# A two-layer graph kernel on one Trainium2 core: another order of ScalarE's work within a step, and the expert product one step later

## The chip, the cores and the metric

The kernel runs on one core of a Trainium2 chip. The metric is the device time in microseconds (us) from launch to end. The profile also gives a span, from the first to the last instruction of one profiled execution. Engines are named as in the profile: PE (matmul), DVE, ACT, POOL, and SP, which issues nearly all DMAs.

## The reference, cut to what matters

Inputs: x of 8 x 1024 x 512, adj of 8 x 1024 x 1024, all float32. The routing picks one of four experts for each of the 8 graphs.

```python
# layer 0
diff = (adj[..., None] - mean_relation) ** 2                 # 4 kernels
w = exp(-0.5 * diff / (1e-14 + precision_relation ** 2))
w = w / sum(w, axis=-1, keepdims=True)                       # over the 4 kernels
ws = sum(w, axis=2)                                          # over the row
x = layernorm(x + reshape(einsum('bknd,nod->bkno', ws[..., None] * x[:, :, None, :], W)))
# layer 1
top1 = argmax(x.mean(axis=1) @ router_w + router_b)
out = einsum('bnm,bmk->bnk', adj, einsum('bnh,bhk->bnk', x, expert_w[top1]))
# batch norm of out with the sums of all graphs that share an expert, gamma, beta, relu
x = layernorm(x + relu(batchnorm(out)))
```

## The kernel before, in words

The 8 graphs have 8 tiles of 128 rows each, so there are 64 tiles (`TILES`). A first part goes through steps n = 0 to `LAST` - 1. Every engine has its own loop over n with the same step numbers, and semaphores alone tie the loops together. In step n:

- SP loads the adj tile n+2 and the x tile n+3, transposes tile n+1 of adj by DMA, stores a finished unit of the expert product from `o_stage` and transposes tile n+2 of x. At a graph's first unit it also loads the chosen expert into `w_sel`.
- POOL cuts the adj tile n+1 and the x tile n+2 into a high and a low float16 half (`pool_al`: adj is cut) and, every second step, normalizes two rows of tiles of x1 (`norm_pair`).
- ACT computes for tile n the squared distances to the four kernels (L513): three into `wgt` and one, SOLO, in place over the adj tile. `weigh_others` takes the exponential of the three in one instruction (L519), `weigh_solo` that of SOLO into the PSUM area `tot` (L524). `sum_reciprocal(n-1)` turns the sum over the four kernels of tile n-1, in the same `tot`, into its reciprocal by a logarithm (L528) and an exponential (L530). ACT also copies two matmul results out of PSUM: a unit of z (L552) and a unit of o (L566).
- DVE: `sums(n)` adds the three weights to `tot` (L781, three instructions). `row_sums(n-1)` multiplies by the reciprocal and sums the rows (L749, three instructions). `weighted(n-1)` adds x and the product h (L768). `low_z` makes the low half of a z unit after ACT's copy (L721), `y_stats`/`y_mean_var` and `o_stats` are statistics (L727, L733, L738).
- PE: `h_product(n)` (12 matmuls), `z_product(n-10)` (24 matmuls; z is adj times x1, 64 units with unit u needing all rows of its graph) and `o_product(n - O_LAG)` (12 matmuls; z times the expert). `z_product(u)` may start when the low half of unit u-2 is made (`dve_z`), `o_product(u)` when unit u-1 was copied out (`act_o`).

`tot` exists once. So `sums(n)` must be finished before `sum_reciprocal(n)`, that before `row_sums(n)`, and that before `weigh_solo(n+1)` and `sums(n+1)`.

After step 63 no adj tiles are left, and PE works off the rest: units 54 to 63 of z and what is left of o. I call this the drain. The last 64 - `KEPT` units of o stay in SBUF, the others go to DRAM (`out_spill`) and come back. When all of o is there, the batch norm constants are made, and a last part goes over the graphs: relu, transposition on PE, addition and layer norm.

Each line number in this text is the one of this kernel.

Of the kernel before, what the change touches and what calls it, by code (L numbers as in the profile page):

```python
# [37 lines left out]
Z_LAG = 10  # L38
O_LAG = 14

# [7 lines left out]
def gnn_program(nc, x, adj, mean_rel, prec_rel, w0, router_w, router_b, expert_w, gamma, beta, x1_spill,  # L48
# [14 lines left out]
    with ExitStack() as ctx:  # L63
# [193 lines left out]
        def _(sp):  # L257
# [54 lines left out]
            for n in range(LAST):  # L312
# [18 lines left out]
                if n + 1 < TILES:  # L331
                    turn_adj(n + 1)
                if 0 <= u - 1 < KEPT:
                    half, k = (u - 1) % T // G, (u - 1) % G
                    sp.wait_ge(act_o, u)
                    dst = out_spill.rearrange("b (c p) n -> b c p n", p=P)[(u - 1) // T, k, :, half * HALF:(half + 1) * HALF]
                    sp.dma_start(dst, o_stage[:, k % 2, :]).then_inc(o_stored[k % 2], 16)
# [14 lines left out]
            def fetch_o(n):  # L352
                i, b = n % RING, batch_of(n)
                if n == 1:

                    sp.wait_ge(o_stored[0], KEPT // 2 * 16 + 16)
                    sp.wait_ge(dve_ws, NK * (TILES - 1))
                    for half in (slice(0, HALF // 2), slice(HALF // 2, HALF)):
                        sp.dma_start(o_chunk(i, 0)[:, half], out_spill[b, 0:P, half]).then_inc(o_back[i], 16)
                elif 1 < n < NB:  # L360
                    if n < RING:

                        sp.wait_ge(pe_z, TILES - T if n == 2 else TILES)
                        if n == 5:

                            sp.wait_ge(pe_h, TILES)
                            sp.wait_ge(pe_o, TILES)
                    else:

                        sp.wait_ge(pe_back, (n - RING + 1) * T)  # L370
                        wait(sp, *landed(o_back, n - RING))

                    for k in range(2):
                        sp.wait_ge(o_stored[k], (b + 1) * T * 8)
                    for h in range(2):
                        src = out_spill.rearrange("b (h c p) n -> b h p c n", h=2, p=P)[b, h]
                        sp.dma_start(o_buf[i][h], src).then_inc(o_back[i], 16)
# [120 lines left out]
        def _(act):  # L498
# [33 lines left out]
            for n in range(LAST):  # L532
# [7 lines left out]
                if 1 <= n <= 2 * E:  # L540
                    e, part_ = expert_half(n - 1)
                    act.wait_ge(experts_landed[e], 16)
                    s.activation(planes(e)[:, 0, part_], expert_in(e)[:, part_], ACT.Copy, scale=W_SCALE).then_inc(act_whi, 1)
                u = n - Z_LAG - 1
                if 0 <= u < TILES:
# [9 lines left out]
                if 0 <= u < TILES:  # L555
# [10 lines left out]
                    s.activation(out_unit(u), ps_out(u), ACT.Copy, scale=1.0 / (Z_SCALE * W_SCALE)).then_inc(act_o, 1)  # L566
                if 0 <= n - 1 < TILES:
                    sum_reciprocal(n - 1)
                if n < TILES:
                    weigh_others(n)  # L570
                    act.wait_ge(pool_al, n + 1)
                    square(n, SOLO, adj_in[:, n % ADJ_RING, :])
                    weigh_solo(n)
# [12 lines left out]
            def relu(n, chunks):  # L586

                i, b = n % RING, batch_of(n)
                if chunks[0] == 0:
                    wait(act, act_o, TILES if n < 2 else 0)  # L590
                    wait(act, *landed(o_back, n))
                pieces = [slice(0, NR)]
# [42 lines left out]
        def _(dve):  # L635
# [147 lines left out]
            for n in range(LAST):  # L783
                if 0 <= n - 2 < TILES:
                    y_stats(n - 2)
                if 0 <= n - Z_LAG - 1 < TILES:
                    low_z(n - Z_LAG - 1)
                if 0 <= n - 2 < TILES:
                    y_mean_var(n - 2)
                if 0 <= n - O_LAG - 1 < TILES:  # L790
                    o_stats(n - O_LAG - 1)
                if 1 <= n <= 2 * E:
# [223 lines left out]
```

## Time and profile before

| | us |
|---|---|
| median of 3 runs | 925.3 (924.48 to 925.61) |
| profiled execution, its own time | 928.54 |
| its span | 926.6 |
| busy in the span: PE, DVE, ACT, POOL | 766.6, 783.0, 799.0, 633.5 |

A busy time says how long an engine had an instruction in work. It does not say which engine the others waited for. That is read from the order of the instructions in one step, where an instruction that had to wait starts right after the end of the one that released it.

### The profile page before, as it was taken

The page shows a single profiled execution, that of the slowest core. Times are in us where ns is not written, and L with a number is a line of the kernel's source. Part 1 is how long each engine was busy: PE and PEld are TensorE (multiplying, and loading weights), DVE is VectorE, ACT ScalarE, POOL GpSimd, SP SyncE. Part 2 cuts the span into 40 slices and gives each one's busy share as a digit, 9 for nine tenths or more (in the row PEclk, how much of TensorE's full clock was granted, in tenths as well). Part 3 has the DMA queues.
Part 4 walks back from the last instruction along what each step waited for, and adds up shares of the span by engine and source line. Part 5 has one row for each costly group of instructions (what it writes and reads, how often), then busy time and mean ns, then how long its engine had stood idle before and what let it go on. Part 6 is the DMA issues. An engine that isn't in the chain of part 4 may idle for free.

```text
span 926.6 us, 12505 instructions
## 1 busy us (share of the span) xinstructions
PE 766.6 (83%) x3922; PEld 362.6 (39%) x3922; DVE 783.0 (84%) x1702; ACT 799.0 (86%) x789; POOL 633.5 (68%) x712
## 2 busy tenths in 40 slices
PE   1445468899999999999999999999999899956652
PEld 1111123344444444444444344444444343425442
DVE  2999988999999999999999999999999712139995
ACT  4999989899999999999999999999999311139997
POOL 7499999999888888888888888888884400000000
PEclk8766679899999999999999999999999989987776
DMA  8599887888797779777877888898763003598896
GB/s 247 150 284 250 184 232 177 218 210 203 197 235 186 182 187 245 201 198 203 208 189 194 222 210 188 199 242 195 191 164 99 1 1 134 198 401 322 295 383 228
DMA packets 262676, 191.17 MB, mean 206 GB/s; under 512 B 210002, under 2 KB 210258, under 8 KB 261074
## 3 DMA queue, kind: packets, MB, share of 16 engines
q1 hardware_dynamic: 262322, 190.38, 74.8%
q8 instruction: 31, 0.51, 0.2%
q14 instruction: 35, 0.29, 0.1%
q10 hardware_dynamic: 288, 0.00, 0.0%
HBM read 91.52 MB, written 48.50 MB: 151 GB/s over the span
## 4 chain that ended last, share of the span: by engine, by line
DVE 49%; ACT 17%; POOL 16%; PE 10%; issue 5%; DMA 2%; SPq 0%; DVEq 0%; POOLq 0%; ACTq 0%
DVE wgt L749 19%; DVE ps_t L781 18%; DVE x_in L768 6%; PE ps_z L929 5%; ACT ps_t L530 4%; ACT ps_t L528 4%; POOL adj_cut L429 3%; PE ps_o L945 3%; POOL x_turn L440 2%; POOL adj_in L424 2%; POOL x1p L466 2%; POOL adj_cut L427 2%; ACT adjT L614 2%; PE ps_t L945 2%; DMA w_sel<-w_planes 1%
## 5 line engine op out<-in xcount | busy, mean ns | idle before, releaser
L929 PE MATMUL ps_z<-adjT,x1p 128*128 128x512 f16 x1536 | 346.5, 383 | 0.0
L914 PE MATMUL ps_h<-w0T,x_turn 128*128 128x512 f16 x768 | 196.3, 410 | 76.9 <-DVE x_in L768 54.1
L781 DVE TENSOR_TENSOR ps_t<-ps_t,wgt 128x1024 f32<-128x1024 f32 x192 | 235.9, 1229 | 15.0 <-ACT ps_t L524 10.6
L749 DVE SCALAR_TENSOR_TENSOR wgt<-wgt,ps_t 128x1024 f32<-128x1024 f32 x192 | 224.8, 1215 | 18.1 <-ACT ps_t L530 17.9
L929 PEld LDWEIGHTS ps_z<-adjT,x1p 128*128 128x128 f16 x1536 | 150.8, 99 | 183.0 <-issue 7.1
L513 ACT ACTIVATE wgt<-adj_in,neg_mu 128x1024 f32<-128x1024 f32 x192 | 205.6, 1134 | 5.5 <-issue 5.4
L519 ACT ACTIVATE wgt<-wgt 128x3072 f32<-128x3072 f32 x64 | 176.5, 2758 | 0.0
L945 PE MATMUL ps_o<-zT,w_sel 128*128 128x512 f16 x684 | 159.9, 384 | 6.2 <-DMA w_sel<-w_planes 6.1
L914 PEld LDWEIGHTS ps_h<-w0T,x_turn 128*128 128x128 f16 x768 | 76.1, 103 | 186.5 <-issue 94.0
L429 POOL TENSOR_TENSOR adj_cut<-adj_in,adj_cut 128x1024 f16<-128x1024 f32 x64 | 136.6, 2134 | 5.3
L492 POOL TENSOR_TENSOR r_nmr<-r_mv,r_std 128x4 f32<-128x4 f32 x16 | 3.2, 199 | 170.7 <-ACT r_std L607 170.7
L945 PEld LDWEIGHTS ps_o<-zT,w_sel 128*128 128x128 f16 x684 | 67.2, 99 | 89.8 <-DMA w_sel<-w_planes 8.7
L424 POOL TENSOR_SCALAR adj_in<-adj_in 128x1024 f32<-128x1024 f32 x64 | 68.7, 1073 | 22.0 <-DMA adj_in<-in_adj_dram 16.9
L552 ACT ACTIVATE zT<-ps_z 128x512 f16<-128x512 f32 x64 | 36.9, 577 | 52.5 <-PE ps_z L929 52.5
L768 DVE SCALAR_TENSOR_TENSOR x_in<-ps_h,wsum,x_in 128x128 f32<-128x128 f32 x256 | 72.6, 344 | 8.9
L721 DVE SCALAR_TENSOR_TENSOR zT<-ps_z,zT 128x512 f16<-128x512 f32 x64 | 43.3, 676 | 43.4 <-ACT zT L552 43.4
L466 POOL TENSOR_TENSOR x1p<-x_in,x1p 128x512 f16<-128x512 f32 x64 | 76.1, 1190 | 5.3
L440 POOL TENSOR_TENSOR x_turn<-x_in,x_turn 128x512 f16<-128x512 f32 x64 | 75.2, 1175 | 5.3
L528 ACT ACTIVATE ps_t<-ps_t 128x1024 f32<-128x1024 f32 x64 | 64.6, 1010 | 10.7 <-DVE ps_t L781 8.7
L513 ACT ACTIVATE adj_in<-adj_in,neg_mu 128x1024 f32<-128x1024 f32 x64 | 72.8, 1138 | 0.0
L427 POOL TENSOR_SCALAR adj_cut<-adj_in 128x1024 f16<-128x1024 f32 x64 | 67.6, 1057 | 5.3
L524 ACT ACTIVATE ps_t<-adj_in 128x1024 f32<-128x1024 f32 x64 | 65.8, 1028 | 2.8 <-DVE wgt L749 0.6
(164 smaller groups left out, 864.0 us busy)
## 6 DMA issues: line engine op xcount, KB each, us to landing
adj_in<-in_adj_dram SPq DMA_DIRECT2D x64, 512.0 KB, 4.0
x_in<-in_x_dram SPq DMA_DIRECT2D x64, 256.0 KB, 4.4
x_spill<-x_in SPq DMA_DIRECT2D x28, 512.0 KB, 3.3
out_spill<-o_stage SPq DMA_DIRECT2D x49, 256.0 KB, 3.0
w_sel<-w_planes SPq DMA_DIRECT2D x8, 1024.0 KB, 6.0
adjT<-x_spill SPq DMA_DIRECT2D x6, 1024.0 KB, 9.6
out_dram<-adjT SPq DMA_DIRECT2D x6, 1024.0 KB, 12.0
adjT<-out_spill SPq DMA_DIRECT2D x4, 1024.0 KB, 9.9
```

What stands on the lines that cost most here:

```text
L429: g.tensor_tensor(cut[:, 1, :], tile, cut[:, 0, :], ALU.subtract).then_inc(pool_al, 1)
L440: g.tensor_tensor(cut[:, 1, :], tile, cut[:, 0, :], ALU.subtract).then_inc(pool_xl, 1)
L466: g.tensor_tensor(x1p[:, b % 2, 1, t, :], row, x1p[:, b % 2, 0, t, :], ALU.subtract).then_inc(pool_1l, 1)
L513: s.activation(to, adj_in[:, n % ADJ_RING, :], ACT.Square, bias=neg_mu[:, k:k + 1], scale=spread[k]).then_inc(act_sq, 1)
L519: s.activation(w, w, ACT.Exp, scale=-1.0).then_inc(act_w, 1)
L528: s.activation(tot, tot, ACT.Ln, scale=SUM_SCALE).then_inc(act_ln, 1)
L749: v.scalar_tensor_tensor(out=wgt[:, m % 2, j, :], in0=wgt[:, m % 2, j, :], scalar=SUM_SCALE / W0_SCALE, in1=tot, op0=ALU.mult, op1=ALU.mul ...
L768: last = v.scalar_tensor_tensor(out=row[:, f], in0=ps_h[:, m % 2, f], scalar=wsum[:, m % 2, COLUMN[k]:COLUMN[k] + 1], in1=row[:, f], op0=A ...
L781: v.tensor_tensor(tot, tot, wgt[:, n % 2, j, :], ALU.add).then_inc(dve_tot, 1)
L914: last = te.matmul(ps_h[:, n % 2, :], xT[:, n % 2, left, c, :], w0T[:, right, c, :], start=(c + i == 0), stop=(c == C - 1 and i == 2))
L929: last = te.matmul(ps_z[:, u % 2, :], x1p[:, b % 2, left, t, k * P:(k + 1) * P], adjT[:, b % 2, right, t, half * HALF:(half + 1) * HALF], ...
L945: last = te.matmul(ps_out(u), w_sel[:, left, c, k * P:(k + 1) * P], zT[:, right, half, c, :], start=(c + i == 0), stop=(c == C - 1 and i = ...
```

## The change

ACT's order within a step becomes: the four squares (SOLO's among them, with its wait for `pool_al`), the logarithm and exponential of `sum_reciprocal(n-1)`, the exponential of the three kernels, the copies of z and o, and the exponential of SOLO, which opens the next tile's sum. `O_LAG` is 15 in place of 14, so that PE, ACT and DVE handle a unit of o one step later, the loop has one more step, and `KEPT` is 48 in place of 49. DVE makes the low half of z and the statistics of o one step later again. SP stores a unit of o one step later relative to its copy. Unit 48 of o stays in SBUF, so the small fetch of `fetch_o(1)` goes away.

```diff
-O_LAG = 14
+O_LAG = 15
...
-                if 0 <= u - 1 < KEPT:
-                    half, k = (u - 1) % T // G, (u - 1) % G
-                    sp.wait_ge(act_o, u)
+                if 0 <= u - 2 < KEPT:
+                    half, k = (u - 2) % T // G, (u - 2) % G
+                    sp.wait_ge(act_o, u - 1)
...
-                if n == 1:
-
-                    sp.wait_ge(o_stored[0], KEPT // 2 * 16 + 16)
-                    sp.wait_ge(dve_ws, NK * (TILES - 1))
-                    for half in (slice(0, HALF // 2), slice(HALF // 2, HALF)):
-                        sp.dma_start(o_chunk(i, 0)[:, half], out_spill[b, 0:P, half]).then_inc(o_back[i], 16)
-                elif 1 < n < NB:
+                if 1 < n < NB:
...
+                if n < TILES:
+                    act.wait_ge(pool_al, n + 1)
+                    square(n, SOLO, adj_in[:, n % ADJ_RING, :])
+                if 0 <= n - 1 < TILES:
+                    sum_reciprocal(n - 1)
+                if n < TILES:
+                    weigh_others(n)
                 u = n - Z_LAG - 1
...
                     s.activation(out_unit(u), ps_out(u), ACT.Copy, scale=1.0 / (Z_SCALE * W_SCALE)).then_inc(act_o, 1)
-                if 0 <= n - 1 < TILES:
-                    sum_reciprocal(n - 1)
                 if n < TILES:
-                    weigh_others(n)
-                    act.wait_ge(pool_al, n + 1)
-                    square(n, SOLO, adj_in[:, n % ADJ_RING, :])
                     weigh_solo(n)
...
-                if 0 <= n - Z_LAG - 1 < TILES:
-                    low_z(n - Z_LAG - 1)
+                if 0 <= n - Z_LAG - 2 < TILES:
+                    low_z(n - Z_LAG - 2)
                 if 0 <= n - 2 < TILES:
                     y_mean_var(n - 2)
-                if 0 <= n - O_LAG - 1 < TILES:
-                    o_stats(n - O_LAG - 1)
+                if 0 <= n - O_LAG - 2 < TILES:
+                    o_stats(n - O_LAG - 2)
```

ACT's queue in the middle of the first part before, one step (the numbers behind L are lines, the arrow goes from what is read to what is written):

```order
L513 ACTIVATE wgt<-adj_in,neg_mu 128x1024 x3
L552 ACTIVATE zT<-ps_z 128x512
L566 ACTIVATE o_stage<-ps_o 128x512
L528 ACTIVATE ps_t<-ps_t 128x1024
L530 ACTIVATE ps_t<-ps_t 128x1024
L519 ACTIVATE wgt<-wgt 128x3072
L513 ACTIVATE adj_in<-adj_in,neg_mu 128x1024
L524 ACTIVATE ps_t<-adj_in 128x1024
```

The same place in the changed kernel, whose lines have other numbers (L506 is the square, L521 and L523 the pair of `sum_reciprocal`, L512 the exponential of three kernels, L517 that of SOLO):

```order
L506 ACTIVATE wgt<-adj_in,neg_mu 128x1024 x3
L506 ACTIVATE adj_in<-adj_in,neg_mu 128x1024
L521 ACTIVATE ps_t<-ps_t 128x1024
L523 ACTIVATE ps_t<-ps_t 128x1024
L512 ACTIVATE wgt<-wgt 128x3072
L552 ACTIVATE zT<-ps_z 128x512
L566 ACTIVATE o_stage<-ps_o 128x512
L517 ACTIVATE ps_t<-adj_in 128x1024
```

The two copies moved from ahead of the pair L528/L530 to behind the large exponential, and SOLO's square from behind that exponential to ahead of the pair.

PE's queue at the end of the first part before, from the second last z product (L929) to the last o product (L945); the fourth row is unit 59 of o:

```order
L929 MATMUL ps_z<-adjT,x1p 128x512 x24
L945 MATMUL ps_o<-zT,w_sel 128x512 x12
L929 MATMUL ps_z<-adjT,x1p 128x512 x24
L945 MATMUL ps_t<-zT,w_sel 128x512 x12
L945 MATMUL ps_o<-zT,w_sel 128x512 x12
L945 MATMUL ps_t<-zT,w_sel 128x512 x12
L945 MATMUL ps_o<-zT,w_sel 128x512 x12
L945 MATMUL ps_t<-zT,w_sel 128x512 x12
```

The same stretch in the changed kernel, where the z product is L924 and the o product L940:

```order
L924 MATMUL ps_z<-adjT,x1p 128x512 x24
L940 MATMUL ps_t<-zT,w_sel 128x512 x12
L924 MATMUL ps_z<-adjT,x1p 128x512 x24
L940 MATMUL ps_o<-zT,w_sel 128x512 x12
L940 MATMUL ps_t<-zT,w_sel 128x512 x12
L940 MATMUL ps_o<-zT,w_sel 128x512 x12
L940 MATMUL ps_t<-zT,w_sel 128x512 x12
L940 MATMUL ps_o<-zT,w_sel 128x512 x12
L940 MATMUL ps_t<-zT,w_sel 128x512 x12
```

Behind the last z product there are now six products of o (units 58 to 63) instead of five.

## Rows read from the trace of the kernel before

**Rows 1.** The page, section 4: the chain that ended last, by engine.

```profile
DVE 49%; ACT 17%; POOL 16%; PE 10%; issue 5%; DMA 2%; SPq 0%; DVEq 0%; POOLq 0%; ACTq 0%
```

**Rows 2.** Windows, 400:700. Busy us (instructions) of the engines, PEclk, DMA.

```profile
core 0: us, PE busy (x) PEld busy (x) DVE busy (x) ACT busy (x) POOL busy (x), PEclk, DMA share, GB/s
400.00:700.00 300.00, 291.89 (x1536) 132.41 (x1535) 287.15 (x596) 296.03 (x274) 263.81 (x288) 1.00 0.80 199
```

**Rows 3.** Timeline of DVE: start, duration, line, tiles, idle before.

```profile
204.25 3.76 DVE L781 TENSOR_TENSOR ps_t<-ps_t,wgt 128x1024 f32<-128x1024 f32 x3
...
210.12 1.22 DVE L749 SCALAR_TENSOR_TENSOR wgt<-wgt,ps_t 128x1024 f32<-128x1024 f32 x1 [0.25 <-ACT ps_t L530]
...
212.41 1.22 DVE L749 SCALAR_TENSOR_TENSOR wgt<-wgt,ps_t 128x1024 f32<-128x1024 f32 x1
...
215.20 3.76 DVE L781 TENSOR_TENSOR ps_t<-ps_t,wgt 128x1024 f32<-128x1024 f32 x3
```

**Rows 4.** Timeline of ACT, step 17.

```profile
203.84 3.21 ACT L513 ACTIVATE wgt<-adj_in,neg_mu 128x1024 f32<-128x1024 f32 x3
206.96 0.57 ACT L552 ACTIVATE zT<-ps_z 128x512 f16<-128x512 f32 x1
207.44 0.58 ACT L566 ACTIVATE o_stage<-ps_o 128x512 f32<-128x512 f32 x1
208.04 1.01 ACT L528 ACTIVATE ps_t<-ps_t 128x1024 f32<-128x1024 f32 x1
...
212.66 1.14 ACT L513 ACTIVATE adj_in<-adj_in,neg_mu 128x1024 f32<-128x1024 f32 x1
213.83 1.03 ACT L524 ACTIVATE ps_t<-adj_in 128x1024 f32<-128x1024 f32 x1
```

**Rows 5.** Timeline of ACT, steps 9, 11, 15 and 16.

```profile
112.76 3.23 ACT L513 ACTIVATE wgt<-adj_in,neg_mu 128x1024 f32<-128x1024 f32 x3
116.86 1.01 ACT L528 ACTIVATE ps_t<-ps_t 128x1024 f32<-128x1024 f32 x1 [0.86 <-DVE ps_t L781]
...
140.24 0.60 ACT L552 ACTIVATE zT<-ps_z 128x512 f16<-128x512 f32 x1 [2.47 <-PE ps_z L929]
140.73 1.02 ACT L528 ACTIVATE ps_t<-ps_t 128x1024 f32<-128x1024 f32 x1
...
185.43 0.60 ACT L566 ACTIVATE o_stage<-ps_o 128x512 f32<-128x512 f32 x1 [1.10 <-PE ps_o L945]
185.92 1.02 ACT L528 ACTIVATE ps_t<-ps_t 128x1024 f32<-128x1024 f32 x1
...
196.59 0.60 ACT L566 ACTIVATE o_stage<-ps_o 128x512 f32<-128x512 f32 x1 [0.22 <-PE ps_o L945]
```

**Rows 6.** Timeline of DVE: the sums of tiles 10 and 14.

```profile
134.97 3.76 DVE L781 TENSOR_TENSOR ps_t<-ps_t,wgt 128x1024 f32<-128x1024 f32 x3
...
181.05 3.76 DVE L781 TENSOR_TENSOR ps_t<-ps_t,wgt 128x1024 f32<-128x1024 f32 x3
```

**Rows 7.** Timeline of POOL: last cut instruction of adj tiles 9 and 17.

```profile
113.94 2.14 POOL L429 TENSOR_TENSOR adj_cut<-adj_in,adj_cut 128x1024 f16<-128x1024 f32 x1
...
197.96 2.13 POOL L429 TENSOR_TENSOR adj_cut<-adj_in,adj_cut 128x1024 f16<-128x1024 f32 x1
```

**Rows 8.** Timeline of PE: unit 0 of o, then the drain.

```profile
181.21 4.18 PE L945 MATMUL ps_o<-zT,w_sel 128*128 128x512 f16 x12 [2.95 <-DMA w_sel<-w_planes]
...
713.19 5.34 PE L929 MATMUL ps_z<-adjT,x1p 128*128 128x512 f16 x24
718.37 2.75 PE L945 MATMUL ps_o<-zT,w_sel 128*128 128x512 f16 x12
720.96 5.34 PE L929 MATMUL ps_z<-adjT,x1p 128*128 128x512 f16 x24
...
740.50 1.01 PE L905 MATMUL ps_s<-ones_h,x1p 128*128 128x1 f16 x32 [3.83 <-POOL x1p L466]
741.37 8.26 PE L929 MATMUL ps_z<-adjT,x1p 128*128 128x512 f16 x24
```

**Rows 9.** Timeline of DVE, step 64: the low half of z.

```profile
725.45 0.67 DVE L721 SCALAR_TENSOR_TENSOR zT<-ps_z,zT 128x512 f16<-128x512 f32 x1
```

More of the change, by code:

```diff
@@ L332, in _ @@
                     turn_adj(n + 1)
-                if 0 <= u - 1 < KEPT:
-                    half, k = (u - 1) % T // G, (u - 1) % G
-                    sp.wait_ge(act_o, u)
-                    dst = out_spill.rearrange("b (c p) n -> b c p n", p=P)[(u - 1) // T, k, :, half * HALF:(half + 1) * HALF]
+                if 0 <= u - 2 < KEPT:
+                    half, k = (u - 2) % T // G, (u - 2) % G
+                    sp.wait_ge(act_o, u - 1)
+                    dst = out_spill.rearrange("b (c p) n -> b c p n", p=P)[(u - 2) // T, k, :, half * HALF:(half + 1) * HALF]
                     sp.dma_start(dst, o_stage[:, k % 2, :]).then_inc(o_stored[k % 2], 16)
@@ L370, in fetch_o @@
                         sp.wait_ge(pe_back, (n - RING + 1) * T)
-                        wait(sp, *landed(o_back, n - RING))
                     for k in range(2):
@@ L590, in relu @@
                     wait(act, act_o, TILES if n < 2 else 0)
-                    wait(act, *landed(o_back, n))
+                    wait(act, o_back[i], n // RING * 32 if n % RING < 2 else 32)
                 pieces = [slice(0, NR)]
```

## The prediction, made before the changed kernel ran

> **What bounds the kernel now.** I began with the chain that ended last: nearly half of it is DVE, with ACT and POOL behind it [rows 1]. The windows view says why the shares alone don't decide: in 300 us of the middle, ACT is busy 296.03, PE 291.89 and DVE 287.15 us, at full granted clock [rows 2]. Three engines are nearly full, so the question is which of them the step's length comes from. I took the order within one step.
>
> The sums on `tot` start at 204.25 and the next ones at 215.20 [rows 3], a step of 10.95 us. Between them lies a ring: sums to the start of the logarithm, 208.04 - 204.25 = 3.79 [rows 3, 4]; the pair L528/L530 until the row sums start, 210.12 - 208.04 = 2.08; row sums and `weighted` until the next sums, 215.20 - 210.12 = 5.08. That makes 10.95 with nothing left over. The small DVE jobs (L727, L721, L733, L738) lie in the 2.08 us in which DVE waits for the reciprocal anyway; 0.25 us of them is still idle [rows 3].
>
> ACT is only just faster. After the copy of o the logarithm starts 208.04 - 207.44 = 0.60 later. Where nothing holds it, it starts 185.92 - 185.43 = 0.49 after the same copy [rows 5]. So ACT waits 0.11 us per step for DVE's sums, and its own ring would be 10.84. PE needs 5.18 for z (718.37 - 713.19) and 2.59 for 12 matmuls (720.96 - 718.37) [rows 8], so 10.36 for h, z and o.
>
> Outside the steady steps there are two places of interest. In steps 11, 15 and 16 ACT waits 2.47, 1.10 and 0.22 for PE before a copy, ahead of the logarithm [rows 5]. In the drain PE alone sets the time.
>
> **The change, part by part.**
>
> *The steady step.* With four squares ahead of it, ACT reaches the logarithm after four pitches of 3.12 / 3 = 1.04 (206.96 - 203.84 is three of them), at 203.84 + 4.16 = 208.00. Today it starts at 208.04, held by the sums that end at 204.25 + 3.76 = 208.01 [rows 3, 4]. Nothing moves. Behind the pair, the two copies (about 0.97 us) take the place of SOLO's square (213.83 - 212.66 = 1.17), so SOLO's exponential could start 0.2 earlier. It is held by the third row sum, which ends at 212.41 + 1.22 = 213.63, and the next sums wait for `weighted`, not for it: it ends at 213.83 + 1.03 = 214.86 and they start at 215.20 [rows 3, 4]. Cost 0. The ring contains no ACT instruction that became shorter.
>
> The 1.17 against 1.04 is worth a look. A square followed by an instruction that reads its result has 0.13 more pitch than a square followed by an unrelated one [rows 4]. The Trainium skill (ScalarE: Activation LUTs, section "What ACT_TABLE_LOAD costs") says that back-to-back ACTIVATEs overlap by about 93 ns, and the trace agrees (duration 1.14, pitch 1.04). By that rule an order without the dependent neighbours would save about 0.1 us in each of 64 steps, some 6 us as an estimate from the Trainium skill; this would count only if ACT set the step.
>
> *The wait for `pool_al`, now earlier.* SOLO's square of tile n now starts 3.12 us into the step. In step 9 that is 112.76 + 3.12 = 115.88, and POOL's cut of tile 9 ends at 113.94 + 2.14 = 116.08 [rows 5, 7]. ACT starts the square at about 116.13, the logarithm at 117.17 instead of 116.86: 0.3 us lost, since this logarithm had followed DVE directly. By step 17 the cut ends at 200.09 and the square is due at 206.96 [rows 4, 7], 6.9 us later, or 3.9 if ACT runs 3 us earlier than today. No further wait.
>
> *The copies, now late in the step.* In step 11 the logarithm starts at 140.73, though the sums of tile 10 had ended by 134.97 + 3.76; with today's latency of 0.03 it could start at 138.76 [rows 5, 6]. In the new order the copy of z comes over 4.5 us later in the step than today, long after PE has delivered. Gain 1.97. In step 15: 185.92 against 181.05 + 3.79 = 184.84, gain 1.08. In step 16 the wait of 0.22 gives about 0.20. Together 3.25; less the 0.3 of step 9, 2.95 us, carried to the end of the first part.
>
> *Low half of z one step later.* `z_product(n-10)` now waits for `low_z(n-12)` in DVE's step n, which ends between the sums' end, 208.01, and the row sums' start, 210.12 [rows 3]; by its place, second of the four small jobs, near 209.2. That is about 2 us behind the place of z in PE's step today. PE's order becomes h, wait, z, o. Once shifted, it needs 10.36 of 10.95 us per step, so it falls behind no further; the small matmuls of routing are inside the 291.89 of 300 us [rows 2]. z runs from 209.2 to 214.4, and its copy comes in ACT's next step, behind the large exponential at about 213.7 + 10.95 - 1.1 = 223.5: 9 us in hand. The o product would start at 214.4, and the copy of o that it waits for ends about when SOLO's exponential starts, at 213.7: 0.7 us to spare, and a miss would cost PE only, which has 0.59 more. Cost 0.
>
> *SP's queue.* The load of `w_sel` moves to an odd step and waits for the last o product of the old graph, which ends about 2 us later in the step; behind it stand the transposes of adj and x and the store of o. The adj transposes are mostly held by POOL's cut anyway, and the store's wait is relaxed by the extra lag. In step 14 PE waited 2.95 us for this load [rows 8]; unit 0 now has a later step. Its gain is that of step 15 above. In the drain, load and product keep their distance. The removed fetch of unit 48 was issued in the drain, long ahead of the last part's second graph, which uses it. Cost 0.
>
> *The drain.* PE makes one o product fewer before step 64 and one more behind it: +2.59 [rows 8]. Against that stands the stall at unit 56 of z, which needs the last rows of x1: PE idles 3.83 us and then takes 8.26 instead of 5.34 for 24 matmuls, 2.92 more [rows 8]. In today's times: z 53 would start some 2 us later than 713.19, by the shift above, so that o 48 ends at 715.3 + 5.18 + 2.59 = 723.1, and z 54 waits for `low_z(52)`, which stands where the low half of unit 53 stands today and ends at 725.45 + 0.67 = 726.12 [rows 9]. PE idles 3 us there. What does the clock do? After an idle of 2.95 us the 12 matmuls at 181.21 took 4.18 instead of 2.75, 1.43 more; after 3.83 us the 24 at 741.37 took 2.92 more [rows 8]. The first is the nearer row in idle time, the second in what runs; I take 1.7. Then z 54 ends at 726.2 + 5.18 + 1.7 = 733.1, o 49 at 735.7, z 55 at 740.9, o 50 at 743.4. The last rows of x1 arrive at 740.5, so there is no idle left at unit 56: routing sums 0.8, z 56 from 744.3 to 749.4. Today it ends at 749.5. The stall is used up by PE's own delay, and the extra product stays: +2.55. With no loss of clock it is 2.55 - 1.7 = +0.85; with 2.92 it is +3.77.
>
> *Last part.* Unchanged. Its first fetches stand in SP's queue behind the last load of `w_sel`, which waits for one o product more (2.59 us), and that load itself lies ahead of ten products more, so they are hidden.
>
> *Sum.* -2.95 + 2.55 = -0.4 us on the span of 926.6, so 926.2. The profiled execution's own time was 928.54, 3.2 above the median of 925.3; the same difference on the median gives **924.9**. Within 0.2% (1.85 us) a measurement of this kernel cannot tell it from no change.
>
> **The rivals.**
>
> *B, the clock holds in the drain.* Then -2.95 + 0.85 = -2.1, 923.2: faster by 0.23%. Against it: an idle of the same length did cost clock at 181.21. For it: 291.89 of 300 us around gaps of 0.6 us show no loss at all [rows 2], and how deep the fall goes differs between my two rows. 16 in 100.
>
> *C, ACT sets the step.* Then 0.13 us less in each of about 62 steps, 8 us, so 925.3 - 0.4 - 8 = 917. This is the case in which the Trainium skill's rule on overlap would decide. Against it: the 0.11 us that ACT waits before the logarithm, and the ring that closes without it. 5 in 100.
>
> *D, PE falls behind (slower).* PE now starts each z behind `low_z` in the same step. Should the idle before z cost clock as at 181.21, a step of PE would be 10.36 + 1.43 = 11.8 us; beyond 10.95 it would first use the 9 us in hand, then set the step: 47 steps by 0.85, less 9, some +30 us, 955. It decides once PE needs more than 10.95. Against it: the spare time per step is only moved, not enlarged. 5 in 100.
>
> *E, the early gain does not come (slower).* POOL is only 0.2 us late in step 9 and cuts at its own pace; if in steps 12 to 16 its cuts, or PE's first z units, hold ACT again, the 3 us are lost and only the drain's term remains: +2.55, 927.9. It needs cuts 2 us later than today's. 10 in 100.
>
> **How the numbers follow.** Forecast 62, B 16, C 5, D 5, E 10; 2 for something faster that I don't see. The forecast's own range, by the drain's bounds, is -2.1 to +0.8. The range that leaves out C, D and half of E, with part of the 1.1 us between the three runs: 922.8 to 927.2. Of the forecast's 62, 60 lie within 0.2%. Faster: B 16, C 5, 2, and 1 of the forecast: 24. Slower: D 5, E 10, 1 of the forecast: 16. Same: 60.
>
> **What the changed profile would show.** Steps of 10.95 us in the middle, as before; no ACT idle before the copies in steps 11, 15, 16, and the squares of step 17 near 200.9 instead of 203.84; a short wait for POOL in step 9; PE waiting for L721's successor before z in most steps; an idle of about 3 us before z 54 and slow matmuls behind it, none before z 56; the last o product ending about 0.4 us earlier than today. Steps shorter than 10.95 would prove C, longer ones D; an end of the first part that is not 3 us earlier, E; a z 54 of 5.3 us, B.

## The result and the profile after

| | before | after |
|---|---|---|
| median (us) | 925.32 (4 runs) | 930.75 (4 runs) |
| ratio to before, 95% interval | | 1.006 (1.0043 to 1.0078) |
| profiled execution, own time | 928.54 | 930.31 |
| its span | 926.6 | 928.4 |

The change made the kernel 5.4 us slower. The forecast was 924.9, between 922.8 and 927.2. It was wrong: the kernel became slower, and by more than the range allowed.

The profiled execution of before that the forecast used spent 3.4 us more in its drain than a second one, profiled later (below). Against that second one the difference of the spans, 5.6 us, is close to the difference of the medians, 5.4. In the table T(n) is the start of SOLO's exponential of tile n, and the drain goes from T(63) to the end of the last o product:

| | before, second profile | after | difference | predicted |
|---|---|---|---|---|
| T(8) | 111.38 | 117.13 | **+5.75** | 0 |
| T(8) to T(17) | 102.09 | 98.86 | **-3.23** | -2.95 |
| T(17) to T(63) | 505.95 | 506.25 | +0.30 | 0 |
| drain | 98.66 | 101.34 | **+2.68** | +2.55 |
| last part | 104.72 | 104.82 | +0.10 | 0 |
| span | 922.8 | 928.4 | +5.6 | -0.4 |

Two of the three large terms came out near the forecast (how much of that was luck is said below). The third, +5.75 up to step 8, was not in the forecast at all. The next rows show where it is made. This is ACT's timeline of the changed kernel in step 2: start, duration, line, operation, and in brackets the idle time ahead of it with what ended it. In the changed kernel L506 are the squares, L521 and L523 the logarithm pair, L512 the large exponential, L517 that of SOLO.

```profile
34.77 1.03 ACT L517 ACTIVATE ps_t<-adj_in 128x1024 f32<-128x1024 f32 x1 [0.97 <-DVE wgt L744]
35.73 3.22 ACT L506 ACTIVATE wgt<-adj_in,neg_mu 128x1024 f32<-128x1024 f32 x3
38.85 1.04 ACT L536 ACTIVATE x1p<-adjT 128x1024 f16<-128x1024 f32 x1
39.80 1.14 ACT L506 ACTIVATE adj_in<-adj_in,neg_mu 128x1024 f32<-128x1024 f32 x1
40.84 1.00 ACT L521 ACTIVATE ps_t<-ps_t 128x1024 f32<-128x1024 f32 x1
41.88 1.01 ACT L523 ACTIVATE ps_t<-ps_t 128x1024 f32<-128x1024 f32 x1
42.80 2.75 ACT L512 ACTIVATE wgt<-wgt 128x3072 f32<-128x3072 f32 x1
46.52 1.03 ACT L517 ACTIVATE ps_t<-adj_in 128x1024 f32<-128x1024 f32 x1 [0.97 <-DVE wgt L744]
```

DVE's timeline of the changed kernel in the same step (L776 sums, L744 row sums):

```profile
36.25 3.76 DVE L776 TENSOR_TENSOR ps_t<-ps_t,wgt 128x1024 f32<-128x1024 f32 x3
...
40.73 1.19 DVE L790 SCALAR_TENSOR_TENSOR x1p<-adjT,x1p 128x1024 f16<-128x1024 f32 x1
42.91 1.22 DVE L744 SCALAR_TENSOR_TENSOR wgt<-wgt,ps_t 128x1024 f32<-128x1024 f32 x1 [0.99 <-ACT ps_t L523]
```

And ACT's timeline of the kernel before in this step:

```profile
35.33 3.21 ACT L513 ACTIVATE wgt<-adj_in,neg_mu 128x1024 f32<-128x1024 f32 x3
38.44 1.04 ACT L543 ACTIVATE x1p<-adjT 128x1024 f16<-128x1024 f32 x1
39.53 1.01 ACT L528 ACTIVATE ps_t<-ps_t 128x1024 f32<-128x1024 f32 x1
40.58 1.01 ACT L530 ACTIVATE ps_t<-ps_t 128x1024 f32<-128x1024 f32 x1
```

In steps 1 to 8 ACT and DVE have one more job. The weights of the four experts are cut into a high and a low float16 part, which I call planes, in two halves per expert: ACT makes the high half (L543 before, L536 after, 1.04 us), DVE the low one, and SP stores the finished planes in `w_planes`. ACT's part stood ahead of the logarithm already. The change puts SOLO's square there too. So five ACT instructions run between the start of the step's squares and the logarithm, 40.84 - 35.73 = 5.11 us, while DVE's sums are done at 36.25 + 3.76 = 40.01. The logarithm is 0.83 late. Row sums, `weighted` and the next sums all follow from it. Nothing fills the place that the square left: ACT idles 0.97 behind the large exponential. The step is 46.52 - 34.77 = 11.75 us instead of 10.95, and the other seven lose 0.7 to 0.9 each. (T(8) shows 5.75 and not the 6.35 that these eight add up to, because tile 0 began 0.60 earlier in this execution, T(0) 21.11 against 21.71.)

Outside these steps the forecast holds. ACT's timeline of the changed kernel in step 11, in step 16, and in a step of the middle (these answer to [rows 5] and [rows 4]):

```profile
148.91 0.59 ACT L552 ACTIVATE zT<-ps_z 128x512 f16<-128x512 f32 x1
149.98 1.03 ACT L517 ACTIVATE ps_t<-adj_in 128x1024 f32<-128x1024 f32 x1 [0.49 <-DVE wgt L744]
...
203.96 0.59 ACT L552 ACTIVATE zT<-ps_z 128x512 f16<-128x512 f32 x1
204.44 0.60 ACT L566 ACTIVATE o_stage<-ps_o 128x512 f32<-128x512 f32 x1
205.04 1.03 ACT L517 ACTIVATE ps_t<-adj_in 128x1024 f32<-128x1024 f32 x1
...
401.83 0.58 ACT L552 ACTIVATE zT<-ps_z 128x512 f16<-128x512 f32 x1
402.30 0.60 ACT L566 ACTIVATE o_stage<-ps_o 128x512 f32<-128x512 f32 x1
402.90 1.03 ACT L517 ACTIVATE ps_t<-adj_in 128x1024 f32<-128x1024 f32 x1
```

No copy waits for PE any more. PE's timeline of the changed kernel, in the middle and in the drain (answers to [rows 8]):

```profile
409.36 5.35 PE L924 MATMUL ps_z<-adjT,x1p 128*128 128x512 f16 x24 [0.21 <-DVE zT L716]
...
728.71 7.04 PE L924 MATMUL ps_z<-adjT,x1p 128*128 128x512 f16 x24 [2.79 <-DVE zT L716]
...
745.94 0.94 PE L900 MATMUL ps_s<-ones_h,x1p 128*128 128x1 f16 x32
746.75 5.34 PE L924 MATMUL ps_z<-adjT,x1p 128*128 128x512 f16 x24
...
792.33 2.76 PE L940 MATMUL ps_o<-zT,w_sel 128*128 128x512 f16 x12 [0.57 <-DMA w_sel<-w_planes]
```

z waits a little for the low half in the middle. z 54 starts after an idle of 2.79 and takes 7.04 instead of 5.34, 1.70 more (the granted clock is 0.54 in its first 3.5 us, near the lower level of 1.2 GHz); the forecast had 3 us and 1.7. Ahead of z 56 there is no idle left (it was 3.83).

### The profile page after: what moved, and what is told of

Read it like the earlier page. It is cut to its first block, busy times and chain, and to the rows that moved or that the text cites. A ratio compares the mean times of both kernels' runs of the same rounds, so it can differ in the third digit from the quotient of the medians.

```text
span 928.4 us, 12501 instructions
## 1 busy us (share of the span) xinstructions
PE 766.2 (83%) x3922; PEld 361.0 (39%) x3922; DVE 784.3 (84%) x1702; ACT 798.8 (86%) x789; POOL 634.5 (68%) x712
## 4 chain that ended last, share of the span: by engine, by line
DVE 53%; ACT 19%; POOL 10%; PE 10%; issue 6%; DMA 1%; DVEq 0%; ACTq 0%; POOLq 0%; SPq 0%
DVE wgt L744 21%; DVE ps_t L776 20%; DVE x_in L763 6%; PE ps_z L924 5%; ACT ps_t L523 5%; ACT ps_t L521 5%; PE ps_t L940 2%; POOL adj_cut L422 2%; PE ps_o L940 2%; ACT adjT L609 2%; POOL x_turn L433 1%; POOL adj_cut L420 1%; ACT x_in L609 1%; POOL adj_in L417 1%; ACT wgt L593 1%
## 5 line engine op out<-in xcount | busy, mean ns | idle before, releaser
L924 PE MATMUL ps_z<-adjT,x1p 128*128 128x512 f16 x1536 | 345.8, 382 | 20.6 <-DVE zT L716 20.4
L909 PE MATMUL ps_h<-w0T,x_turn 128*128 128x512 f16 x768 | 197.6, 412 | 74.7 <-DVE x_in L763 59.5
L776 DVE TENSOR_TENSOR ps_t<-ps_t,wgt 128x1024 f32<-128x1024 f32 x192 | 235.9, 1229 | 14.8 <-ACT ps_t L517 10.4
L744 DVE SCALAR_TENSOR_TENSOR wgt<-wgt,ps_t 128x1024 f32<-128x1024 f32 x192 | 224.8, 1216 | 22.6 <-ACT ps_t L523 22.6
L924 PEld LDWEIGHTS ps_z<-adjT,x1p 128*128 128x128 f16 x1536 | 146.9, 98 | 212.7 <-DVE zT L716 40.8
L506 ACT ACTIVATE wgt<-adj_in,neg_mu 128x1024 f32<-128x1024 f32 x192 | 205.8, 1136 | 5.9 <-issue 5.9
L512 ACT ACTIVATE wgt<-wgt 128x3072 f32<-128x3072 f32 x64 | 176.5, 2759 | 0.0
L940 PE MATMUL ps_o<-zT,w_sel 128*128 128x512 f16 x672 | 154.2, 379 | 0.6 <-DMA w_sel<-w_planes 0.6
L909 PEld LDWEIGHTS ps_h<-w0T,x_turn 128*128 128x128 f16 x768 | 78.0, 104 | 180.9 <-issue 91.2
L940 PEld LDWEIGHTS ps_o<-zT,w_sel 128*128 128x128 f16 x672 | 65.6, 98 | 80.1 <-DMA w_sel<-w_planes 1.1
L417 POOL TENSOR_SCALAR adj_in<-adj_in 128x1024 f32<-128x1024 f32 x64 | 67.0, 1047 | 21.0 <-DMA adj_in<-in_adj_dram 15.8
L517 ACT ACTIVATE ps_t<-adj_in 128x1024 f32<-128x1024 f32 x64 | 65.8, 1028 | 13.7 <-DVE wgt L744 12.4
L506 ACT ACTIVATE adj_in<-adj_in,neg_mu 128x1024 f32<-128x1024 f32 x64 | 72.7, 1136 | 0.0
L521 ACT ACTIVATE ps_t<-ps_t 128x1024 f32<-128x1024 f32 x64 | 64.5, 1008 | 8.0 <-DVE ps_t L776 5.8
## 6 DMA issues: line engine op xcount, KB each, us to landing
out_dram<-adjT SPq DMA_DIRECT2D x6, 1024.0 KB, 11.3
```

What stands on the lines that cost most here:

```text
L506: s.activation(to, adj_in[:, n % ADJ_RING, :], ACT.Square, bias=neg_mu[:, k:k + 1], scale=spread[k]).then_inc(act_sq, 1)
L512: s.activation(w, w, ACT.Exp, scale=-1.0).then_inc(act_w, 1)
L521: s.activation(tot, tot, ACT.Ln, scale=SUM_SCALE).then_inc(act_ln, 1)
L744: v.scalar_tensor_tensor(out=wgt[:, m % 2, j, :], in0=wgt[:, m % 2, j, :], scalar=SUM_SCALE / W0_SCALE, in1=tot, op0=ALU.mult, op1=ALU.mul ...
L776: v.tensor_tensor(tot, tot, wgt[:, n % 2, j, :], ALU.add).then_inc(dve_tot, 1)
L909: last = te.matmul(ps_h[:, n % 2, :], xT[:, n % 2, left, c, :], w0T[:, right, c, :], start=(c + i == 0), stop=(c == C - 1 and i == 2))
```

## The experiments

All medians stand beside runs of the kernel before on the same chip, 925.3 to 925.9. T(n) and the drain are as above and those of the profiled execution.

**The kernel before, profiled a second time.**

> The kernel before, unchanged, looked at once more. The profiled execution that the prediction used took 928.5 us, 3.2 above the median; in its drain PE waited 2.2 us for the last w_sel load and then ran the o product in 4.25 us. Theory 1: this wait and the slow stretch behind it come and go with the landing time of the load, so another look whose own time is near 925.3 shows an idle under 1 us there and an o product of about 2.75. Rival: the 3.2 us lie elsewhere (start or last part), and the wait is 2.2 us again.

Median 925.34. Its profile shows the drain at 98.66 instead of 102.04: the wait for the last `w_sel` was 0.88 instead of 2.21, and the o product behind it took 2.76 instead of 4.25. Step 11 waited 3.72 for PE, and steps 15 and 16 not at all; the total of the three, 3.79 in the forecast's trace, is about the same. The start and the last part differ by less than 0.5 us, so the rival has fallen.

**SOLO's square late in steps 0 to 8** (from the changed kernel).

```diff
-                if n < TILES:
+                if 2 * E < n < TILES:
                     act.wait_ge(pool_al, n + 1)
                     square(n, SOLO, adj_in[:, n % ADJ_RING, :])
...
                     weigh_others(n)
+                if n <= 2 * E:
+                    act.wait_ge(pool_al, n + 1)
+                    square(n, SOLO, adj_in[:, n % ADJ_RING, :])
```

> The changed kernel, but in steps 0 to 8 the square of SOLO stands behind the large exponential again, as before. Theory 1 (the loss is the pile of three squares, half an expert plane and SOLO's square ahead of the logarithm in steps 1 to 8): steps 1 to 8 are 10.95 us again instead of 11.75, the whole is 5.4 us below the changed kernel, at 925.3, ratio to before about 1.000. Rival (the earlier wait for POOL's cut in these steps holds ACT, or the longer lag costs all of it in the drain): no more than 1 us below the changed kernel, ratio 1.005 or more.

Median 924.06, ratio 0.9979 (0.9963 to 0.9995). ACT's timeline of this kernel in step 2:

```profile
39.09 1.04 ACT L536 ACTIVATE x1p<-adjT 128x1024 f16<-128x1024 f32 x1
40.18 1.01 ACT L521 ACTIVATE ps_t<-ps_t 128x1024 f32<-128x1024 f32 x1
...
45.96 1.03 ACT L517 ACTIVATE ps_t<-adj_in 128x1024 f32<-128x1024 f32 x1
```

The steps are 10.95 again (45.96 - 35.01), T(8) is 112.07, T(63) 717.23: 5.0 earlier than in the changed kernel, and the median 6.7 lower, more than the 5.4 expected. With the one place mended, the change is 1.3 us faster than before. Both rivals have fallen.

**SOLO's square early in steps 1 to 8** (from the kernel before, nothing else changed).

```diff
+                if 1 <= n <= 2 * E:
+                    act.wait_ge(pool_al, n + 1)
+                    square(n, SOLO, adj_in[:, n % ADJ_RING, :])
...
                 if 0 <= n - 1 < TILES:
                     sum_reciprocal(n - 1)
                 if n < TILES:
                     weigh_others(n)
-                    act.wait_ge(pool_al, n + 1)
-                    square(n, SOLO, adj_in[:, n % ADJ_RING, :])
+                    if not 1 <= n <= 2 * E:
+                        act.wait_ge(pool_al, n + 1)
+                        square(n, SOLO, adj_in[:, n % ADJ_RING, :])
```

> The kernel before, with one part of the change alone: in steps 1 to 8 SOLO's square stands ahead of the logarithm. Theory 1: 0.8 us more in each of the eight steps, less 0.6 for a wait in step 8 that the kernel before has anyway: 5.4 us at the end of step 8; some of it may be hidden in step 11, where ACT waits 2.5 us for PE, if PE is not pushed back with it. So 928.5 to 930.7, ratio 1.0035 to 1.006. Rival (the loss comes from the lag): ratio 1.000.

Median 928.28, ratio 1.0028 (1.0012 to 1.0044). T(8) is 117.71, the loss in full, so the rival, the lag, didn't make it. But T(63) is only 3.2 later than in the second profile of before. ACT's timeline of this kernel in step 11:

```profile
143.79 0.57 ACT L555 ACTIVATE zT<-ps_z 128x512 f16<-128x512 f32 x1
144.87 1.01 ACT L528 ACTIVATE ps_t<-ps_t 128x1024 f32<-128x1024 f32 x1 [0.51 <-DVE ps_t L785]
```

The copy of z waits for nothing: PE's first z had time to finish while ACT was late. PE's timeline shows it, first of the kernel before (second profile), then of this one (L905 and L909 are the sums for the routing, which need the same last rows of x1 as z 0):

```profile
132.21 1.01 PE L905 MATMUL ps_s<-ones_h,x1p 128*128 128x1 f16 x32 [3.36 <-POOL x1p L466]
133.08 8.05 PE L929 MATMUL ps_z<-adjT,x1p 128*128 128x512 f16 x24
```

```profile
135.44 1.02 PE L909 MATMUL ps_s<-ones_h,x1p 128*128 128x1 f16 x32
136.32 5.34 PE L933 MATMUL ps_z<-adjT,x1p 128*128 128x512 f16 x24
```

Before, PE idled for POOL's last rows of x1 and then ran z 0 at a granted clock of 0.50 (133 to 136 us), until 141.13. Here z 0 starts 3.2 later, without that idle, takes 5.34 and ends at 141.66, only 0.5 later, while ACT is 6.3 later. So the loss and the gain are not two independent things. The wait of step 11 absorbs about 3 us of the delay made before it, and where a delay has already hidden it, removing the wait brings almost nothing: T(63) is 722.59 here and 722.24 in the changed kernel.

**The lags alone** (the changed kernel with ACT's old order).

```diff
-                if n < TILES:
-                    act.wait_ge(pool_al, n + 1)
-                    square(n, SOLO, adj_in[:, n % ADJ_RING, :])
-                if 0 <= n - 1 < TILES:
-                    sum_reciprocal(n - 1)
-                if n < TILES:
-                    weigh_others(n)
...
+                if 0 <= n - 1 < TILES:
+                    sum_reciprocal(n - 1)
                 if n < TILES:
+                    weigh_others(n)
+                    act.wait_ge(pool_al, n + 1)
+                    square(n, SOLO, adj_in[:, n % ADJ_RING, :])
                     weigh_solo(n)
```

> The changed kernel with ACT's order of before: only the lag of 15 and the later low halves and statistics are left. Theory 1: steps 1 to 8 at 10.95 us; the wait of step 11 is back (2.5 us), those of steps 15 and 16 stay away (-1.3); drain +2.6: together +1.3 us against before, 926.6, ratio 1.001. Rival (the lag and the later low half of z cost most of the 5.4 us): 929 or more, ratio 1.004 or more.

Median 927.62, ratio 1.0021 (1.0006 to 1.0035). ACT's timeline of this kernel:

```profile
140.58 0.60 ACT L545 ACTIVATE zT<-ps_z 128x512 f16<-128x512 f32 x1 [2.67 <-PE ps_z L922]
...
196.48 0.60 ACT L559 ACTIVATE o_stage<-ps_o 128x512 f32<-128x512 f32 x1 [0.86 <-PE ps_o L938]
```

T(63) is 719.91, as before, and the drain 101.17: the lags alone cost the drain its 2.5 us and nothing else, and the waits for PE stay. The expectation had those of steps 15 and 16 gone; one of 0.86 stayed, and the time is 1.0 above the 926.6 expected. So ACT's order is what removes these waits, and what makes the loss.

**Step 11 alone in the new order** (from the kernel before: the copy of z 0 behind the large exponential, its low half in the next step).

```diff
+                if n == Z_LAG + 1:
+                    act.wait_ge(pool_al, n + 1)
+                    square(n, SOLO, adj_in[:, n % ADJ_RING, :])
...
                     weigh_others(n)
+                    if n == Z_LAG + 1:
+                        copy_z(0)
```

> The kernel before with one thing else: in step 11 alone ACT uses the new order (SOLO's square early, the copy of z unit 0 behind the large exponential), and DVE makes that unit's low half in step 12. Theory 1 (the gain at the end of the first part in the changed kernel comes from two waits of ACT for PE, the larger in step 11): the wait of 2.5 to 3.7 us there goes, the first part ends 2 to 3 us earlier, 922.5 to 923.3, ratio 0.997 to 0.998. Rival (PE is behind for good, and the wait comes back in a later step): ratio 1.000.

Median 924.36, ratio 0.998 (0.9963 to 0.9997). The wait of step 11 is gone (T(11) 145.36) and comes back in step 15, 3.12 us before the copy of o 0, whose product waits for the first load of `w_sel`. That is the rival's course. T(16) is 203.84, later than in the second profile of before: in this trace nothing is gained. But the profiled execution took 928.04, the longest of the twelve, so it doesn't speak for the median, which is a little lower than before and still 1.1 above the range expected.

**The same, and the first `w_sel` load one step of SP earlier.**

```diff
+                if n == O_LAG - 1:
+                    load_w(0)
```

> As defer_z0, and the first w_sel load is issued one step earlier, at the end of SP's step 13, ahead of the step 14 store of x1 that waits for POOL. Theory 1: PE's wait before unit 0 of o and ACT's waits in steps 15 and 16 are gone in every execution; they were there in one of two looks at the kernel before (1.3 us). So 0 to 1.3 us below defer_z0, 921.5 to 923, ratio 0.9965. Rival: the load collides with the adj and x loads of step 14 and gives it back: ratio as defer_z0.

Median 923.68, ratio 0.9977 (0.996 to 0.9993). No ACT wait for PE is left, T(16) is 199.71, 2.8 earlier than in the second profile of before, T(63) 716.66. That settles what the early gain of the change is: these waits, worth 2.8 to 3.3 us in the first part. The median shows only 1.9 of it and misses the range expected by 0.7. Its profiled drain had a last load of `w_sel` that came 2.16 late, with the o product at 4.37.

**A second buffer for the last expert** (from the kernel before; the load goes into the area of the adj ring, free by then, and waits for no o product).

```diff
-                    wait(sp, pe_o, u)
+                    if m < NB - 1:
+                        wait(sp, pe_o, u)
...
+                    if m == NB - 1:
+                        sp.wait_ge(act_solo, TILES)
...
-                    sp.dma_start(w_sel[:], w_planes[e]).then_inc(w_landed, 16)
+                    sp.dma_start(w_of(m), w_planes[e]).then_inc(w_landed, 16)
```

> The kernel before, with the last graph's expert loaded into the adj tiles' area, which is free by then, so that the load does not wait for the last o product of the graph before. Theory 1: PE's idle before unit 56 of o (2.2 us with 1.6 us of slow clock behind it in the first look, 0.9 without in the second) is gone: 0.9 to 3.9 us, 921.5 to 924.4, ratio 0.996 to 0.999. Rival (the fetches for the last part, which now start earlier as well, take its place or slow the load): ratio 1.000.

Median 924.71, ratio 0.9988 (0.9976 to 1.0001); the drain of the profiled execution is 96.35, 2.3 shorter than in the second profile of before, with no wait at the o product. Only 0.9 of that is the wait; 1.2 is z 56, which took 6.66 here and 7.89 there after the same idle of 3.83. The median is 0.8 below that of before on the same chip, 925.54, and 0.3 above the range expected, and the interval still holds "no change".

**The three together.**

> The kernel before with the three edits of defer_z0, pe_waits_off and second_w_buffer. If they add up as theory 1 has it: 2.5 + 0.6 + 1.5 = 4.6 us, 920.7, ratio 0.995. If one of them only moves a wait: 923 or more.

Median 921.37, ratio 0.9954 (0.9934 to 0.9974), T(16) 199.54, drain 97.39. It is the fastest version here, 4 us faster than before, with ACT's old order in every step but step 11.

**The expert plane late instead of the square** (from the changed kernel: L536 moved behind the large exponential, DVE's half and the plane's store one step later).

```diff
                 if n < TILES:
                     weigh_others(n)
+                if 1 <= n <= 2 * E:
+                    e, part_ = expert_half(n - 1)
+                    act.wait_ge(experts_landed[e], 16)
+                    s.activation(planes(e)[:, 0, part_], ...)
...
-                if n in (3, 5, 7, 9):
-                    e = (n - 3) // 2
+                if n in (4, 6, 8, 10):
+                    e = (n - 4) // 2
```

> The changed kernel with one thing else: in steps 1 to 8 ScalarE makes its half of the expert plane (1.04 us) behind the exponential of three kernels instead of ahead of the logarithm; VectorE's half and the plane's store go a step later. The square of SOLO stays early. Theory 1 (the chain of steps 1 to 8 is three squares, plane half, SOLO's square, logarithm pair, exponential, wait for the row sum; the early square costs 0.8 there only because the plane half stands ahead of the logarithm too): the steps are 10.95 long again instead of 11.75, the SOLO exponential of step 8 starts near 112 instead of 117.1, step 16 near 200, the median near 924 (ratio 0.998). Rival (the early square itself costs, by GpSimd's pool_al or by VectorE, wherever the plane stands): steps of 11.75 and about 930 as the changed kernel.

Median 927.11, ratio 1.0014 (0.9999 to 1.003), halfway between the two theories. T(8) is 110.63: the loss of the first steps is gone, with SOLO's square still early, so the rival that the early square itself costs has fallen. But T(11) is 147.17. ACT's timeline of this kernel in step 11:

```profile
146.67 0.60 ACT L552 ACTIVATE zT<-ps_z 128x512 f16<-128x512 f32 x1 [3.48 <-DMA w_planes<-zT]
```

The copy of z 0 writes `zT`, in which the last plane was made, and waits for its store. SP's own timeline of this kernel shows that store late, at 140.83 (125.95 in the changed kernel):

```profile
140.83 0.58 SPq L345 DMA_DIRECT2D w_planes<-zT  x1
```

**The same, with that store in step 9.**

```diff
-                if n in (4, 6, 8, 10):
-                    e = (n - 4) // 2
+                if n in (4, 6, 8, 9):
+                    e = (n - 3) // 2
```

> The kernel with the expert plane behind the large exponential, and the store of the last plane issued in SP's step 9 instead of step 10. In the version before this one the steps 1 to 8 were 10.95 long (SOLO exponential of step 8 at 110.63, against 117.13 in the changed kernel), but the copy of the first z waited 3.48 for the store of the last plane, which reads the buffer that the copy writes: it was issued at 140.83, in the changed kernel at 125.95. Theory 1: with the store some 10 us earlier that wait is gone, or what is left of it is a short wait for PE's first z; the SOLO exponential of step 16 starts near 199 to 200, the median is 923.5 to 924.5, as with SOLO's square late. Rival: the wait of 3.48 was PE's (z of unit 0 under the slow clock) and stays; then 927.1 again.

Median 924.87, ratio 0.9992 (0.9979 to 1.0005), 5.9 below the changed kernel. ACT's timeline of this kernel in step 2:

```profile
38.12 1.13 ACT L506 ACTIVATE adj_in<-adj_in,neg_mu 128x1024 f32<-128x1024 f32 x1
39.31 1.01 ACT L521 ACTIVATE ps_t<-ps_t 128x1024 f32<-128x1024 f32 x1
...
43.92 1.05 ACT L543 ACTIVATE x1p<-adjT 128x1024 f16<-128x1024 f32 x1
44.99 1.03 ACT L517 ACTIVATE ps_t<-adj_in 128x1024 f32<-128x1024 f32 x1
```

The store went out at 130.46 and the wait of 3.48 is gone, so it was the store's and not PE's. T(8) is 111.36, T(16) 199.68, T(63) 716.76, 5.5 before the changed kernel. The median is 0.4 above the range expected, less than half the width of its interval. So either of the two instructions may stand ahead of the logarithm in steps 1 to 8, but not both.

**Half the dose: SOLO's square late in steps 5 to 8 only.**

```diff
-                if n < TILES:
+                if n < TILES and not E < n <= 2 * E:
                     act.wait_ge(pool_al, n + 1)
                     square(n, SOLO, adj_in[:, n % ADJ_RING, :])
...
                     weigh_others(n)
+                if E < n <= 2 * E:
+                    act.wait_ge(pool_al, n + 1)
+                    square(n, SOLO, adj_in[:, n % ADJ_RING, :])
```

> The changed kernel with the square of SOLO behind the exponential of three kernels in steps 5 to 8 only, so half the dose of the all-eight version. Theory 1 (each of the steps 1 to 8 costs 0.8 for itself): steps 1 to 4 are 11.75, the SOLO exponential of step 4 starts near 70.1, steps 5 to 8 are 10.95, that of step 8 starts near 114.2, 2.9 before the changed kernel; the drain unchanged, the median near 927.5 (ratio about 1.002). Rival (a loss made once, at the start or at the change of the form): either all or nothing of the 5 us between the two versions comes back, 924 or 930.7.

Median 927.1, ratio 1.0021 (1.0006 to 1.0036), between 924.06 and 930.75. T(4) is 70.16 as in the changed kernel, and the next steps lose less, so each step costs for itself. But T(8) is 115.17, not 114.2. DVE's timeline of this kernel in step 8:

```profile
105.28 3.76 DVE L779 TENSOR_TENSOR ps_t<-ps_t,wgt 128x1024 f32<-128x1024 f32 x3
...
109.76 1.89 DVE L793 SCALAR_TENSOR_TENSOR zT<-w_sel,zT 128x1024 f16<-128x1024 f32 x1
111.58 1.21 DVE L747 SCALAR_TENSOR_TENSOR wgt<-wgt,ps_t 128x1024 f32<-128x1024 f32 x1
```

Here the low half of the plane (L793) takes 1.89 instead of the 1.19 of step 2 and holds the row sums, which could start at 110.11 + 1.01. Three steps are 11.3 long for that reason. POOL's timeline of this kernel shows what goes with the stretch:

```profile
109.54 1.05 POOL L417 TENSOR_SCALAR adj_in<-adj_in 128x1024 f32<-128x1024 f32 x1
```

L793 starts while POOL's L417 has 0.83 us to go and ends 1.06 after that one's end (109.54 + 1.05 = 110.59). It is the same for all 41 low halves of a plane longer than 1.3 us in the fourteen traces: each began while a POOL instruction had 0.24 us or more to go, and ended 1.06 to 1.09 after that instruction's end. So DVE seems to wait there for POOL's instruction; no run moves POOL's work to prove it. The kernel before has such a step too, 95 us into its first profile: a low half of 2.15, and a step of 11.52.

**The changed kernel once more.**

> The changed kernel once more, unchanged, beside the other two on the same chip. All theories: 930.3 to 931.2 (ratio 1.006), SOLO exponential of step 8 near 117.1 and of step 63 near 722.2. If it comes out near 927, the size of the slowdown differs from execution to execution and the ratio of the first comparison is to be taken with that spread.

Median 930.76, ratio 1.0047 (1.003 to 1.0065): the size of the slowdown is confirmed. Its profiled execution divides it otherwise: T(63) is 723.41, 1.2 later (T(4) was already 1.1 later), and the drain 99.55, 1.8 shorter. PE's timeline of this execution shows why the drain is shorter:

```profile
729.88 5.35 PE L924 MATMUL ps_z<-adjT,x1p 128*128 128x512 f16 x24 [2.80 <-DVE zT L716]
```

The same idle as at 728.71 above, and no slow clock behind it.

## Why the prediction was wrong

**The step that failed** is "the steady step", cost 0. Its working is right for the steps it was read from: four pitches of 1.04 bring ACT to the logarithm just when the sums end. But the sum used it for all 64 steps, as a cost of 0. In steps 1 to 8 a fifth instruction, the expert plane of L543, stands in the same place, and there the 0.03 us of slack becomes 0.8 us of loss per step. L543 stood in the trace of before, at 38.44; the argument never looked at a step before 9. The early square put alone into the kernel before makes the whole loss at T(8) (117.71). Two mends at different ends, the square late (924.06) and the plane late (924.87), each give it back, and half a dose gives part of it.

**Rightly forecast:** the gain of steps 11, 15 and 16 (-2.95 forecast; T(8) to T(17) is 3.1 shorter with the late square, where no early delay helps). The +0.3 of step 9 didn't come, since by then ACT was 5 us later than assumed, and POOL's cut was done. Where ACT isn't late, with the late square, the wait is there, but smaller: the square of step 9 starts at 116.39, POOL's cut ends at 116.36, and the step is 11.06, 0.1 longer. The drain: +2.55 forecast, +2.68 found, with z 54 and z 56 as described and 101.17 against 98.66 with the lags alone. The mechanism was right; that the number agrees to 0.1 is partly luck. The 1.7 us of slow clock at z 54 came in four of seven profiled executions. In the repetition it didn't, and the drain was 99.55, +0.89, next to the forecast's own +0.85 for that case. The steady step: 10.95 before and after. The +0.30 between T(17) and T(63) is mostly one step of 11.22 (402.90 to 414.12), which isn't explained.

**The sum.** The stretches of the table add up, but what each part of the change is worth by itself does not. With SOLO's square early and the rest as before, T(8) to T(17) is 98.94; in the changed kernel it is 98.86, in the changed kernel with the late square 98.96, and before 102.09. So the new place of the copies does bring the 3.2 us, but a delay of 5 to 6 us ahead of them shortens the stretch by the same 3.2. Once the early steps lose 5.75, all that the copies' place could gain is gone, which is why mending the loss brings 5.0 at T(63) with the square late.

**The rivals.** None took place as the cause. B's mechanism, a clock that holds in the drain, happened in some executions (below), but B's time was 923.2. C fell: the square of SOLO and the exponential that reads it stand apart now, and the step is still 10.95. So the estimate of 6 us from the Trainium skill (ScalarE: Activation LUTs, "What ACT_TABLE_LOAD costs") did not come, though the overlap is there: in step 2 SOLO's square to the next instruction is 40.84 - 39.80 = 1.04 now. In the middle the logarithm behind it is held by DVE's sums. D fell: z waits 0.21 in the middle and takes 5.35. E fell: the 3 us weren't lost to POOL or PE in steps 12 to 16. Its sign, a first part that doesn't end 3 us earlier (T(63) 722.24 against 719.42), did show, and its time, 927.9, was nearer than the forecast, but by another mechanism. The case "slower because an engine is late in a stretch with an extra job" was missing from the list.

**The offset.** The forecast scaled from a profiled execution 3.2 above the median. The second profile shows what most of these 3 us were: the late load of `w_sel` and the slow product behind it. It did no harm here, since the term of the drain didn't rest on it.

## What to carry to other kernels

A step in a loop with start-up jobs is several steps: before an instruction is moved, list what stands ahead of the critical one in each kind of step, and compute the slack in each. Where slack is a few hundredths of a us, one more instruction there costs nearly its length in every such step (0.8 of 1.04 here). And a wait that a change removes may be what hides another delay: gains and losses that meet at the same wait are not added.

## What the runs showed of the hardware

- The same idle of PE costs clock in some executions and little or none in others. z 54 after an idle of 2.79 or 2.80 us took 7.04, 7.04, 6.88 and 6.77 in four profiled executions of the lagged kernels, and 5.35 in three; the mean granted clock from 720 to 800 us was 0.98 in the first four and 1.00 in the other three. The windows view of the changed kernel and of its repetition:

```profile
720.00:800.00 80.00, 76.64 (x382) 34.46 (x381) 29.99 (x83) 15.61 (x24) 10.46 (x14) 0.98 0.16 60
```

```profile
720.00:800.00 80.00, 76.73 (x390) 34.95 (x389) 31.08 (x85) 17.09 (x25) 11.49 (x17) 1.00 0.19 70
```

- The idle of 3.83 to 3.85 us ahead of z 56 always cost clock, but not always the same: the 24 matmuls took 6.66 to 8.26 instead of 5.34 in the seven profiled executions of kernels with the old lag.
- A late load can be paid twice. PE's timeline of the kernel before, the forecast's execution and the second profile:

```profile
783.75 4.25 PE L945 MATMUL ps_o<-zT,w_sel 128*128 128x512 f16 x12 [2.21 <-DMA w_sel<-w_planes]
```

```profile
781.64 2.76 PE L945 MATMUL ps_o<-zT,w_sel 128*128 128x512 f16 x12 [0.88 <-DMA w_sel<-w_planes]
```

The wait for the load was 1.3 longer and the product behind it took 1.5 longer (granted clock 0.63 against 1.00), so one DMA landing late made 2.8 of the 3.4 us between the drains of two executions of one kernel. At the first and the last load of `w_sel`, waits of 1.75 and 1.94 left the 12 matmuls at 2.76, and eight waits of 2.10 to 3.75 made them 4.18 to 4.45.
